# Attention scores of four heads by three passes of 32-row tiles, and TensorE's share of the row sums in quarters

## What is computed

```python
q = _layernorm_scale_only(q, q_ln_scale); k = _layernorm_scale_only(k, k_ln_scale)
scores = jnp.einsum('bshd,bthd->bhst', q / jnp.sqrt(jnp.float32(HEAD_DIM)), k)
scores = jnp.where(causal, NEG_INF, scores)
attn = jax.nn.softmax(scores, axis=-1)
ctx = jnp.einsum('bhst,bthd->bshd', attn, v)
```

## Time and profile before

| | us |
|---|---|
| median of 3 runs | 2472.2 |
| lowest, highest | 2464.5, 2473.1 |
| the profiled execution | 2468.9 |
| its span, first to last instruction | 2467.1 |
| TensorE, VectorE, ScalarE, GpSimd busy in it | 2364.6, 1784.9, 1315.8, 277.7 |

### The profile page before, as it was taken

One profiled execution on the slowest core, in us unless ns is written; L12 is line 12 of the kernel. 1 busy time (PEld: TensorE's weight loads), 2 busy tenths in 40 slices (PEclk: granted clock), 3 DMA queues, 4 the chain that ended last, 5 costly groups with the idle time before them and its releaser, 6 DMA issues. The chain is left out here.

```text
span 2467.1 us, 37850 instructions
## 1 busy us (share of the span) xinstructions
PE 2364.6 (96%) x12546; PEld 1408.4 (57%) x12546; DVE 1784.9 (72%) x1821; ACT 1315.8 (53%) x1631; POOL 277.7 (11%) x266
## 2 busy tenths in 40 slices
PE   8999967999999999999999999959999999999997
PEld 7777743433333333333334333338888888888885
DVE  7666665898978989689897898964556465555654
ACT  4444435888878888688888888821111111111111
POOL 1111111210122111221112211100000000000000
PEclk9999977999999999899999999979999999999999
DMA  7766676010640106311055110063021111110100
GB/s 245 242 225 239 213 220 133 23 31 5 122 100 23 32 6 117 93 35 31 6 99 118 28 31 6 6 220 121 18 69 35 36 52 32 55 39 31 35 18 17
DMA packets 126429, 197.67 MB, mean 80 GB/s; under 512 B 14992, under 2 KB 39568, under 8 KB 126224
## 3 DMA queue, kind: packets, MB, share of 16 engines
q1 hardware_dynamic: 126224, 195.10, 28.2%
HBM read 122.70 MB, written 72.35 MB: 79 GB/s over the span
## 5 line engine op out<-in xcount | busy, mean ns | idle before, releaser
L884 ACT ACTIVATE probs<-score 128x1024 f32<-128x1024 f32 (+3 forms) x1152 | 1024.2, 956 | 227.2 <-PE score L801 220.6
L950 DVE TENSOR_TENSOR total<-total,probs 128x2048 f32<-128x2048 f32 (+3 forms) x472 | 981.9, 2080 | 67.6 <-POOL probs L762 32.2
L801 PE MATMUL score<-qstk,kstk 98*128 98x512 f32 (+3 forms) x2304 | 666.0, 411 | 41.0 <-DMA kstk<-k_hi 16.6
L801 PEld LDWEIGHTS score<-qstk,kstk 98*128 98x128 f32 x2304 | 383.5, 192 | 538.1 <-ACT probs L884 437.1
L817 PE MATMUL ctx_acc<-probs,values 128*32 128x512 f32 (+3 forms) x4608 | 581.5, 577 | 7.4 <-POOL probs L762 6.7
L1289 ACT ACTIVATE hidden<-slot,gate_scale_sb 128x512 f32<-128x512 f32 x128 | 88.1, 688 | 625.2 <-PE slot L1218 625.2
L762 POOL TENSOR_SCALAR_AFFINE_SELECT probs<-probs 128x512 f32<-128x512 f32 x128 | 199.7, 1561 | 1042.9 <-ACT probs L884 1042.9
L1374 DVE SCALAR_TENSOR_TENSOR hidden<-slot,up_scale_sb,hidden 128x512 f32<-128x512 f32 x128 | 96.1, 751 | 261.4 <-ACT hidden L1289 261.4
L817 PEld LDWEIGHTS ctx_acc<-probs,values 128*32 128x32 f32 x4608 | 91.8, 108 | 203.8 <-issue 163.9
L1218 PE MATMUL slot<-xt_hi,wg_sb 128*128 128x512 f32 x512 | 201.6, 394 | 5.3 <-issue 5.3
L1229 PE MATMUL y<-wd_sb,h_hi 128*128 128x512 f32 x512 | 199.4, 389 | 1.4 <-DVE h_lo L1382 1.4
(11 more groups left out here) (101 smaller groups left out, 1982.4 us busy)
## 6 DMA issues: line engine op xcount, KB each, us to landing
qstk<-q_hi SPq DMA_DIRECT2D x64, 256.0 KB
kstk<-k_hi SPq DMA_DIRECT2D x64, 256.0 KB, 8.9
wq_int<-in_wq SPq DMA_DIRECT2D x48, 256.0 KB, 3.1
wq_float<-wq_f SPq DMA_DIRECT2D x48, 256.0 KB, 2.7
x_raw<-in_x_t SPq DMA_DIRECT2D x32, 256.0 KB, 3.4
v_rows<-v_out SPq DMA_DIRECT2D x32, 256.0 KB, 2.1
q_hi<-part_hi SPq DMA_DIRECT2D x32, 256.0 KB, 2.2
q_lo<-part_lo SPq DMA_DIRECT2D x32, 256.0 KB, 2.5
```

What stands on the lines that cost most here:

```text
L801: ins = pe.matmul(score[u % RING][:, i, cut(t):], kstk[0:ROWS, h, kb * P:(kb + 1) * P], qstk[0:ROWS, q_buffer[ch], h, cut(t):], start=True ...
L884: act.activation(probs[:, t % PB, 2 * p:2 * p + 2, cut(t):], score[u % RING][:, :, cut(t):], ACT.Exp).then_inc(exped, 1)
L950: dve.tensor_tensor(into, into, now, ALU.add).then_inc(added, 1)
```

## The change

- `kstk` and `qstk` become `keys` and `queries`: the four heads of a group take 32 partitions each, and the coarse and the fine part stand side by side; nothing is stored twice. The loads are two of 256 KB for a piece of keys or queries, instead of three. The rows of shifts have a tensor of their own, loaded by two small transfers (`shift_load`), and are used only under the flag. The memsets of ones into `kstk` go.
- `scores`: for each of the three products four matmuls of 32 rows, one a head, each on its own 32 rows of the array and into its own PSUM bank; the three passes add up in PSUM. All twelve follow one wait, and the signal to ScalarE comes once, after the last.
- `by_pe` becomes `own`: on the fourth, eighth, twelfth ... step of a chunk (from chunk 1 on, 35 in a group) TensorE sums the last 128 of the 512 columns and VectorE adds the other 384. VectorE skips no step. The closing sum of such a chunk is done for 384 and 128 columns apart.
- TensorE's stream stands twice, for flag on and off, behind `If` and `Else`.

Nothing changes on ScalarE but the counts that it waits for, nor in `project` and `finish`.

```diff
 def attend(nc, io, dr, keep):
+    PARTS = ((0, 0), (1, 0), (0, 1))
...
+    SUM = P
+    SUMMED = 3
...
-    def by_pe(t):
+    def own(t):
         ch, kb = steps[t]
-        return not diagonal(t) and t - first[ch] >= ST * 2 and (t - first[ch]) % 10 == 0
+        return CH - SUM if not diagonal(t) and t - first[ch] > 1 and (t - first[ch]) % 4 == SUMMED else CH
...
-        kstk = sb("kstk", [P, HG, S], F32R)
-        qstk = sb("qstk", [P, 3, HG, CH], F32R)
+        keys = sb("keys", [P, 2, S], F32R)
+        queries = sb("queries", [P, 3, 2, CH], F32R)
+        shift = sb("shift_rows", [P, 3, CH], F32R)
+        one_rows = sb("one_rows", [P, P], F32R)
...
         def k_load(sp, g, j, s):
-            for r, src in enumerate(("k_hi", "k_lo", "k_hi")):
+            for a, src in enumerate(("k_hi", "k_lo")):
...
         def q_load(sp, g, ch, b, s):
-            for r, src in enumerate(("q_hi", "q_hi", "q_lo")):
+            for a, src in enumerate(("q_hi", "q_lo")):
...
+        def shift_load(sp, g, ch, b, s):
+            for a in range(2):
+                sp.dma_start(shift[a:P:HD, b, :].bitcast(F32),
...
-            def scores(g, t):
+            def scores(g, t, shifted):
...
-                for p in range(2):
-                    u = 2 * t + p
-                    pe.wait_ge(exped, 2 * NS * g + u + 1)
-                    for i in range(2):
-                        h = 2 * p + i
-                        ins = pe.matmul(score[u % RING][:, i, cut(t):], kstk[0:ROWS, h, kb * P:(kb + 1) * P],
-                                        qstk[0:ROWS, q_buffer[ch], h, cut(t):], start=True, stop=True)
-                    ins.then_inc(scored, 1)
+                pe.wait_ge(exped, 2 * NS * g + 2 * t + 2)
+                b = q_buffer[ch]
+                for q, k in PARTS:
+                    for h in range(HG):
+                        rows = slice(h * HD, (h + 1) * HD)
+                        ins = pe.matmul(score[(2 * t + h // 2) % RING][:, h % 2, cut(t):], keys[rows, k, kb * P:(kb + 1) * P],
+                                        queries[rows, b, q, cut(t):], start=(q, k) == PARTS[0],
+                                        stop=(q, k) == PARTS[-1] and not shifted)
...
+                ins.then_inc(scored, 2)
...
-                if by_pe(t):
+                if own(t) < CH:
...
-                        ins = pe.matmul(sums[h * HD:(h + 1) * HD, n0:], ones[:], probs[:, t % PB, h, n0:],
+                        ins = pe.matmul(sums[h * HD:(h + 1) * HD, own(t):], ones[:], probs[:, t % PB, h, own(t):],
                                         start=opens, stop=False)
...
-                for h in range(HG):
-                    ins = pe.matmul(sums[h * HD:(h + 1) * HD, :], ones[:], total[:, ch % 2, h, :], start=opens, stop=True)
+                for part in (slice(0, CH),) if opens else (slice(0, CH - SUM), slice(CH - SUM, CH)):
+                    for h in range(HG):
+                        ins = pe.matmul(sums[h * HD:(h + 1) * HD, part], ones[:], total[:, ch % 2, h, part], start=opens,
+                                        stop=part.stop == CH)
...
-                    if not by_pe(t) and (place or not ch):
+                    if place or not ch:
...
-                        now = probs[:, t % PB, :, cut(t):]
-                        into = total[:, ch % 2, :, cut(t):]
+                        now = probs[:, t % PB, :, cut(t):own(t)]
+                        into = total[:, ch % 2, :, cut(t):own(t)]
```

More of the change, by code:

```diff
@@ L545, in diagonal @@
         return steps[t][1] >= ST * steps[t][0]
[L547 removed]
+    def own(t):
         ch, kb = steps[t]
[L550 to L553 removed]
+        return CH - SUM if not diagonal(t) and t - first[ch] > 1 and (t - first[ch]) % 4 == SUMMED else CH
+    NA = NS
     assert NS % PB == 0 and 2 * NS % RING == 0
     NM = sum(diagonal(t) for t in range(NS))
[L557 to L558 removed]
     def masks_before(t):
@@ L782, in _ @@
                     pe.wait_ge(g_split, g + 2)
+            pe.wait_ge(ones_ready, 2)
             pe.sem_inc(scored, Q_CREDIT)
@@ L818, in weigh @@
                                     probs[:, t % PB, h, n0:], start=t in first, stop=t in last)
-                if by_pe(t):
-                    opens = not any(by_pe(x) for x in range(first[ch], t))
+                if own(t) < CH:
+                    opens = not any(own(x) < CH for x in range(first[ch], t))
                     if opens:
@@ L829, in sum_total @@
             def sum_total(g, ch):
-                opens = not any(by_pe(x) for x in range(first[ch], last[ch] + 1))
+                opens = not any(own(x) < CH for x in range(first[ch], last[ch] + 1))
                 if opens:
                     pe.wait_ge(sums_taken, NCH * g + ch + 1)
-                pe.wait_ge(added, NA * g + adds_before(last[ch] + 1) + A_CREDIT)
-                for h in range(HG):
-                    ins = pe.matmul(sums[h * HD:(h + 1) * HD, :], ones[:], total[:, ch % 2, h, :], start=opens, stop=True)
@@ L837, in sum_total @@
-                ins.then_inc(totaled, 1)
[L839 to L852, removed]
@@ new lines, in sum_total, with program, group @@
+                ins.then_inc(totaled, 1)
+            def program(shifted):
+                def group(g, after):
+                    for t in range(NS):
+                        if t + LAG < NS:
+                            scores(g, t + LAG, shifted)
+                        elif after:
+                            scores(g + 1, t + LAG - NS, shifted)
+                        weigh(g, t)
+                        if t + LAG - T_LAG in last:
+                            sum_total(g, last.index(t + LAG - T_LAG))
+                    sum_total(g, NCH - 1)
+                for t in range(LAG):
+                    scores(0, t, shifted)
+                with pe.Fori(0, NG - 1) as g:
+                    group(g, True)
+                group(NG - 1, False)
@@ L857, in _ @@
+            with pe.If(general):
+                program(True)
+            with pe.Else():
+                program(False)
         @block.scalar
```

47 lines of the change are left out of this document (24 added, 23 removed).

## The result

The changed kernel takes **2531.6 us** (median of 4 runs, 2527.8 to 2534.2) against 2468.6 before (4 runs, 2464.5 to 2473.1): a ratio of 1.0257, 95% interval 1.0232 to 1.0281. The forecast was 2437, with 2418 to 2500 as its range. The sign was wrong, and the size is off by 95 us.

The account below looks back on a forecast made before the run. TensorE was taken as the bound, VectorE close behind. From 2468.9 us profiled, -24 for four groups, -13 for loads and +2 for branches gave 2434, or 2437 on the median; 8-in-10 range 2418 to 2500.

Parts of the forecast that it names:

- Row sums: TensorE's row sums per group: 10 steps with whole sums (2.98 us) become 35 with quarter sums of 0.25 us.
- Batch of four row tiles: Scores: four 32-row matmuls overlap fully, so a batch costs 0.225 us (bounds 0.213 to 0.43).
- The first rival: Scores: weights can't load under a matmul on the same rows, passes two and three pay 0.11 each; 2541, 13 in 100.
- Ring: Attention step: scores wait for the previous step's first exponential, one signal releases ScalarE; plain step 2.12 to 2.08 us.
- After a narrow step: Full-step scores followed by weighing of a 128-column step: 1.48 us becomes 2.08, 8 per group, +4.8 us.
- With a quarter sum: Steps carrying a quarter sum: TensorE needs 1.90 + 0.25 = 2.15 us, over 2.08.
- With a closing sum: Seven steps per group with a chunk's closing sum: 3.00 to 2.78 us, -1.5 us a group.
- The groups: Attention: step changes sum to -6 us a group, -24 us for four groups.
- Loads: First group: 2.9 MB fewer copies at 206 GB/s shorten the 16.4 us wait before the third chunk to 3; -13 us.
- Branch: Loop's branch back: more instructions per step, so the queue covers less time; +2 us for three branches (0 to 6).
- VectorE in the long chunk: Longest chunk, 32 steps: VectorE's work 65.2 us against about 66 for the chunk; costs nothing now, leaves no room.
- partial overlap: Scores: row tiles overlap only in part, step cycle 2.29 us; total 2541, 13 in 100.

Follow-up runs that it names:

- the early copy: Changed kernel, but VectorE copies the last chunk's row sums out after its addition of the third step, not the fifth: 2433.7 us, ratio 0.9854.
- the skewed kernel: The early copy with scores in two pairs of heads, the second one pass behind, two waits and two signals: 2412.6 us, ratio 0.9784.
- the kernel with old scores: Kernel before with only the row-sum change (quarter sums, split closing sum), its 98-row scores and loads kept: 2571.9 us, ratio 1.0421.

## Why the prediction was wrong

**The step that failed is "Row sums".** It costed 35 steps with a quarter sum at 0.25 us of TensorE each and looked at nothing but the streaming. Seven of the 35 do one thing more: they open `sums_acc`, and an opening waits for VectorE's copy of the last chunk's sums. The diff moves it from place 10 (in the second chunk from the closing sum) to place 3, without a line of the diff at the wait itself. It was to be seen in the trace before: additions of 2.3 us back to back, a copy put behind the fifth of a chunk, hence done some 3 us after the fourth step is weighed. With the 3.5 us that a stall was measured to cost, the missing term is 4 x 7 x 3.5 = +98. With it the forecast is 2535, and the kernel took 2531.6. The trace before could give the wait, not the half-speed stretches behind it.

**The rest of the sum**, read in the kernel with the early copy, where that wait is gone (profiled span 2434.0; before 2467.1):

- Batch of four row tiles: taken 0.225, measured 0.23 apart, the four starts within 10 ns. Two rows of the changed kernel's timeline, the first pass's four matmuls and the eight weight loads of the passes after it:

```profile
1583.64 0.50 PE L807 MATMUL score<-queries,keys 32*128 32x512 f32 x4
...
1583.75 0.42 PEld L807 LDWEIGHTS score<-queries,keys 32*128 32x128 f32 x8
```

  The first rival (rows that can't be loaded under a matmul on the same rows) is refuted by its own condition: the next loads begin 0.11 us after the first pass, while it streams on those rows. So the rule of the Trainium skill, page "TensorE: Matmul & The Clock Gate", section "Part 3: Packing small matmuls — row/col tiling", by which weight loads overlap only where the row group differs, is not what this trace shows. (The same section also lets a load run ahead that targets the background weight buffer; the sentence with "only" leaves that case out.) Its 3.07 times for four tiles is not seen in a row of three batches either: from one batch to the next it is 0.34 once and then 0.23, and 0.23 for four tiles is what one full-array matmul took the earlier trace rows.
- Ring: plain step 2.08 forecast, 2.10 measured. After a narrow step 2.08, measured 2.10. With a quarter sum 2.15, measured 2.12. With a closing sum 2.78, measured 2.76. ScalarE's wait 0.14, measured 0.15. All this holds from the second group on. In the first group a plain step takes 2.18 and ScalarE waits 0.24:

```profile
626.29 0.97 PE L807 MATMUL score<-queries,keys 32*128 32x512 f32 x12 [0.22 <-ACT probs L904]
...
627.39 1.94 ACT L904 ACTIVATE probs<-score 128x1024 f32<-128x1024 f32 x2 [0.24 <-PE score L807]
...
628.47 0.97 PE L807 MATMUL score<-queries,keys 32*128 32x512 f32 x12 [0.22 <-ACT probs L904]
```

  The changed kernel and the early copy both have it; a plain step of the kernel before takes 2.12 in every group. Through it the first group's last six chunks are 7.8 us longer than the second's. Its cause is open.
- The groups: -6 us each forecast. From first scores to first scores the second and third group are 5.7 and 7.8 shorter. The first is 20.0 shorter, but 19.8 of that is its second chunk (16.2 us for 36.0), which belongs to the loads; its other chunks, with steps of 2.18, bring 0.2. The last group is 0.5 shorter from its first to its last scores. Its second chunk is 3.9 longer (19.5 for 15.6, with one wait of 2.28 for an exponential and 3.4 us at half speed), which the later ones give back. Then its end costs 3.7 more: TensorE, done with weighing, waits 3.73 us for VectorE's last addition where it waited 0.40, and streams the closing sum at half speed. Kernel before, then early copy:

```profile
1620.21 1.07 PE L836 MATMUL sums_acc<-total,ones 128*32 128x512 f32 x8 [0.40 <-DVE total L950]
```

```profile
1585.05 1.94 PE L848 MATMUL sums_acc<-total,ones 128*32 128x384 f32 x16 [3.73 <-DVE total L969]
```

  The prediction let VectorE fall behind in a long chunk and catch up in the next one; behind the last chunk there is no next one.
- Loads: -13 was too small. The first scores come 3.9 earlier (353.1 for 357.0), and the first group's second chunk is 19.8 shorter: -24 together. The rate was taken as a constant of 206 GB/s; it belonged to the layout, and the new one reaches 333 to 359. The stall of 16.4 us before the third chunk is gone, not cut to 3. The other 3.4 go along with the clock: before, it was granted at half speed until 376.6 us, now until 362.2.
- Branch: +2 forecast for three branches. There are two, and their gaps are 3.32 and 2.52 for 2.57 and 2.06: +1, contained in the groups above.
- VectorE in the long chunk: 65.2 us of work against 66 for the ring, which measured 66.9 (68.9 in the first group). An addition of 1536 columns was taken as 1.79, give 1.76, and it measured 1.78. With no wait VectorE would indeed be next; the skewed kernel runs into it.

Sum: -4 ahead of the attention, -30 in it, +1 behind, -33 where -35 was forecast. That it fits to 2 us is luck: the loads brought 24 where 13 was forecast, the groups with their branches 10 where 22 was, and the two errors of some 11 us cancel. The term that was left out is nearly three times the whole sum.

**The rivals** were all about how fast the tiles are. The one of a slowdown with the most weight, partial overlap at 2541, gives nearly the measured time by a mechanism that isn't there: the score matmuls and the waits, not the total, tell them apart.

## What to carry to other kernels

When a change moves a first write into a shared accumulator or buffer, look for the `wait` that only the first writer makes and for the place of the reader that frees it; both can stand outside the diff. Place such a copy by when its reader can make it, ahead of the long operations queued on its engine: two steps earlier, with not one operation saved, were worth 98 us here. A total that fits is no proof of its terms: compare group by group, and look at the first and the last one by themselves. And where one signal for a whole step closes a ring, splitting it can pay even if it adds to the bound engine, provided that the parts overlap.

## What the runs showed of the hardware

- Row tiles of two pairs run as two independent rows: with the second pair 0.19 us behind, each keeps 0.34 and 0.23 between its passes. Four tiles need not be issued in step.
- A stall of 2.3 us on a TensorE that is otherwise some 93% busy was followed in about two of three cases by a granted clock of 1.2 GHz for 3.4 or 6.8 us; of the 24 stalls of 0.5 us at the same steps, from the third chunk on, none was, and both stalls of 2.1 us in that kernel were. It is not certain for a single stall, in the kernel with old scores no more than in the changed one: there scores behind one such stall took 2.08 us, behind another 1.21.
- In the stretches in which keys and queries were loaded into 32 partitions with four pieces of 2 KB each, 209 GB/s were moved, into 128 partitions with one piece of 2 KB each 359 GB/s, both at a DMA share of 1.1.
